# A decoder of two layers on one core: the projections of causal and full attention as three passes of rounded and rest parts

## The chip, the cores and the metric

The kernel runs on one core of one Trainium2 chip. The metric is the device time of one execution in microseconds, the median of the runs. TensorE (PE) multiplies, VectorE (DVE), ScalarE (ACT) and GpSimd (POOL) work element by element, and DMAs are issued from the queues of SyncE (SP) and POOL.

## The reference

The input x is 4 sequences of 512 tokens and 256 channels, in 32-bit floats. Six blocks follow each other, each on a layer norm of x and added to x:

```python
x = x + causal_attention(ln(x))         # 16 heads of 16, rope factor on q and k, projection + bias
x = x + geglu(ln(x), ctx)
x = x + routed_ffn(ln(x))               # 8 experts, top 2, and a shared one
x = x + full_attention(ln(x))           # 16 heads of 16
x = x + cross_attention(ln(x), ctx)     # softmax over the queries
x = x + routed_ffn2(ln(x))              # 8 experts of 1024
```

The two self attentions compute `qkv = x @ W.T + b`, softmax of `q k / 4`, times v, and `y @ W_out.T + b_out`. A projection in them is the product with `W` (256 x 768) or `W_out` (256 x 256).

## The kernel before

`attention` runs twice: once for the causal attention (tiles named l0a, four batches of 512 tokens), and once for full and cross attention together (l1a, batches 0 to 3 full, 4 to 7 cross). Each batch has four groups of four heads. A schedule written out by hand (`attention_slot`, L95) gives the order for all engines: one slot for a batch and group, in a slot eight steps j. Each step has the scores by key (`S`, L758) and, for a later group, the scores by query (`A`, L721), whose row maximum DVE takes (L539); ACT takes the exponential of S (L644). Scores use three PSUM buffers in turn: an S or A waits until the reader of the score three places before is done. `PV` (L783) multiplies probabilities with v; `Z` (L792) turns the result by tokens, DVE divides it (L547, L551), and `N` (L800) turns it back once for each pair of groups.

Everything else on PE shares one PSUM bank, `m_ps`: `take_m` makes the next writer wait for the reader of the last one. The work for the next batch sits in slots 0 and 1 of this one: `PREP` uses 0 and 1 transpose the normed x (L687; read by ACT, L604, into `xnT`), uses 2 to 5 are the four q and k chunks of 128 channels by 512 tokens (L698, two matmuls of 512 columns each), uses 6 and 7 are v (L707, two token tiles each, two matmuls of 256 columns for each tile). `OUT` (L809) is the output projection, two matmuls of 256 columns, read by DVE (L563), which adds it to x. It comes twice for each pair of groups, four times for a batch; pair 0 of a batch is projected in its slot 2, pair 1 in slot 0 of the next batch. So slot 0 has, one behind the other on `m_ps`: PREP 0 (step 3), N (step 4), PREP 1 (step 4), OUT (step 5), PREP 2 (step 6), OUT and PREP 3 (step 7).

A matmul on 32-bit operands is two records in the trace (each with a weight load). Operands that a rounding wrote as F32R are multiplied in one; the scores already work so, from `hi` and `lo` stacked along the contraction. Routed layers do three passes, hi times hi, hi times lo and lo times hi (helper at L1783 with 256 columns each).

A batch of index 0 is prepared before the loop: its PREP steps stand at the start of the stage, with score buffers in place of `m_ps`. Behind them SP issues the 48 DMAs that stack q (L393), then the row maxima of group 0 (L399); the first S waits for these.

## Time and profile before

| | us |
|---|---|
| median of 3 runs | 1979.07 (1970.0 to 1981.77) |
| the profiled execution's own time | 1973.59 |
| its span | 1971.8 |
| causal stage, first instruction to last | 9 to 316 |
| full attention, first to its last projections | 794 to 1152 |

The profiled execution has a mean granted TensorE clock of 0.878 of 2.4 GHz. In the 2.4 us between span and time nothing of the kernel runs. Of a view by windows, one line is a stretch of the span; the sums of engines overlap, so a stretch is as long as the chain of waits in it, not as the busiest engine. A record's length of a matmul holds its latency; the rate of a stream is the distance between starts.

### The profile page before, as it was taken

The numbers are of one execution on the slowest core, as the hardware profiler recorded it, in microseconds if no ns is written. First come the engines' busy times: TensorE is split into PE (matmuls) and PEld (weight loads), VectorE is DVE, ScalarE is ACT, GpSimd is POOL, SyncE is SP. The second block draws the span as 40 slices with busy tenths as digits, with TensorE's granted clock in tenths as the row PEclk, the third lists the DMA queues.
The fourth block names the chain that finished last, engine by engine and source line by source line (L and its number), as shares of the span: only waits on it lengthen the run. The fifth ranks groups of instructions, "written<-read, shape, count | busy, mean of one in ns | idle before, by whom it ended". The sixth has DMA issues, their size and how long they took to land. (4 is left out here: it accounts for less than half of the span.)

```text
span 1971.8 us, 32181 instructions
## 1 busy us (share of the span) xinstructions
PE 1569.6 (80%) x11072; PEld 1117.7 (57%) x11072; DVE 1191.7 (60%) x2003; ACT 932.7 (47%) x1745; POOL 609.2 (31%) x887
## 2 busy tenths in 40 slices
PE   4789986855969996378888977877760799999996
PEld 2455443555969996233333322322240799999996
DVE  3555553451458885377677467575743477787773
ACT  1344452121346663036546556466721466666662
POOL 5243420015004443624334343233015221222222
PEclk8799998956989998679999997676755899999998
DMA  5122211163058985434232222122015567777763
GB/s 142 25 52 51 49 34 33 53 168 112 28 155 235 232 232 127 117 77 96 45 80 60 61 41 52 34 55 40 9 44 174 158 202 213 219 204 201 210 193 80
DMA packets 211537, 216.56 MB, mean 110 GB/s; under 512 B 33393, under 2 KB 187378, under 8 KB 211346
## 3 DMA queue, kind: packets, MB, share of 16 engines
q1 hardware_dynamic: 176626, 175.10, 30.2%
q0 software_dynamic: 34752, 39.43, 11.3%
q8 instruction: 88, 1.44, 0.3%
q14 instruction: 71, 0.58, 0.1%
HBM read 139.48 MB, written 38.96 MB: 90 GB/s over the span
## 5 line engine op out<-in xcount | busy, mean ns | idle before, releaser
L638 ACT ACTIVATE l1a_sb_probs<-l1a_s_ps,l1a_sb_kmax 128x512 f32<-128x512 f32 x256 | 173.1, 684 | 95.9 <-issue 72.8
L1783 PE MATMUL l1m_xg_ps<-l1m_sb_xrows_hi,l1m_sb_hi 128*128 128x256 f32 x736 | 209.2, 284 | 1.4 <-DVE l1m_sb_xrows_lo L1705 1.4
L1783 PE MATMUL l1m_xg_ps<-l1m_sb_xrows_hi,l1m_sb_lo 128*128 128x256 f32 x736 | 208.9, 284 | 0.0
L1783 PE MATMUL l1m_xg_ps<-l1m_sb_xrows_lo,l1m_sb_hi 128*128 128x256 f32 x736 | 208.8, 284 | 0.0
L445 POOL DMA_DIRECT2D l1a_sb_kst<-l1a_sb_hi x256 | 125.5, 494 | 267.8 <-PE l1a_s_ps L758 236.3
L573 DVE TENSOR_REDUCE l1a_sb_kmax<-l1a_s_ps 128x2 f32<-128x1024 f32 x128 | 155.3, 1220 | 83.4 <-PE l1a_s_ps L758 83.3
L539 DVE TENSOR_REDUCE l1a_sb_mx<-l1a_s_ps 128x2 f32<-128x1024 f32 x128 | 154.1, 1219 | 75.2 <-PE l1a_s_ps L721 75.1
L1629 POOL DMA_INDIRECT sum_dram<-l1m_sb_xy,l1m_sb_xnote x46 | 79.8, 1734 | 322.5 <-DVE l1m_sb_xy L1755 315.5
L644 ACT ACTIVATE l1a_sb_probs<-l1a_s_ps 128x1024 f32<-128x1024 f32 x128 | 128.0, 1022 | 104.7 <-PE l1a_s_ps L758 104.5
L539 DVE TENSOR_REDUCE l0a_sb_mx<-l0a_s_ps 128x2 f32<-128x256 f32 (+3 forms) x128 | 103.4, 821 | 93.6 <-PE l0a_s_ps L732 92.2
L758 PEld LDWEIGHTS l1a_s_ps<-l1a_sb_qst,l1a_sb_kst 49*128 49x128 f32 (+1 forms) x512 | 51.6, 211 | 166.6 <-issue 102.6
L758 PE MATMUL l1a_s_ps<-l1a_sb_qst,l1a_sb_kst 49*128 49x512 f32 (+1 forms) x512 | 129.9, 534 | 18.3 <-issue 17.6
L1783 PEld LDWEIGHTS l1m_xg_ps<-l1m_sb_xrows_hi,l1m_sb_hi 128*128 128x128 f32 x736 | 141.9, 193 | 1.8 <-DVE l1m_sb_xrows_lo L1705 1.8
L1783 PEld LDWEIGHTS l1m_xg_ps<-l1m_sb_xrows_hi,l1m_sb_lo 128*128 128x128 f32 x736 | 142.0, 193 | 0.0
L1783 PEld LDWEIGHTS l1m_xg_ps<-l1m_sb_xrows_lo,l1m_sb_hi 128*128 128x128 f32 x736 | 141.9, 193 | 0.0
L1711 DVE TENSOR_TENSOR l1m_sb_lo<-l1m_sb_raw,l1m_sb_hi 128x512 fp32r<-128x512 f32 x184 | 119.9, 693 | 32.6 <-ACT l1m_sb_hi L1664 21.3
L783 PE MATMUL l1a_o_ps<-l1a_sb_probs,l1a_sb_vscaled 128*32 128x512 f32 x512 | 92.8, 805 | 58.0 <-DVE l1a_sb_vscaled L591 47.4
L644 ACT ACTIVATE l0a_sb_probs<-l0a_s_ps 128x1024 f32<-128x1024 f32 (+3 forms) x128 | 87.3, 698 | 78.3 <-PE l0a_s_ps L732 78.1
L1629 POOL DMA_INDIRECT sum_dram<-l0m_sb_xy,l0m_sb_xnote x46 | 79.4, 1726 | 137.6 <-DVE l0m_sb_xy L1755 127.6
L1664 ACT ACTIVATE l1m_sb_hi<-l1m_sb_raw 128x512 fp32r<-128x512 f32 x184 | 105.0, 620 | 16.4 <-DMA l1m_sb_raw<-in_l1m_w 16.2
L1783 PE MATMUL l1m_xy_ps<-l1m_sb_hi,l1m_sb_xh_hi 128*128 128x256 f32 x368 | 106.7, 290 | 2.8 <-issue 2.8
L1783 PE MATMUL l0m_xg_ps<-l0m_sb_xrows_hi,l0m_sb_hi 128*128 128x256 f32 x368 | 105.5, 287 | 2.7 <-DVE l0m_sb_xrows_lo L1705 2.7
(332 smaller groups left out, 4199.1 us busy)
## 6 DMA issues: line engine op xcount, KB each, us to landing
l1m_sb_raw<-in_l1m_w SPq DMA_DIRECT2D x184, 256.0 KB
l0m_sb_raw<-in_l0m_w SPq DMA_DIRECT2D x96, 256.0 KB
l1m_sb_raw<-in_l1m_w SPq DMA_DIRECT2D x23, 1024.0 KB
l0m_sb_raw<-in_l0m_w SPq DMA_DIRECT2D x24, 512.0 KB
l1a_sb_qst<-l1a_sb_hi SPq DMA_DIRECT2D x256, 32.0 KB, 2.3
l1a_sb_kst<-l1a_sb_hi POOLq DMA_DIRECT2D x256, 32.0 KB, 2.0
rows_dram<-const_blank SPq DMA_DIRECT2D x2, 2967.0 KB, 24.1
l0m_sb_xrows<-rows_dram SPq DMA_DIRECT2D x23, 258.0 KB, 4.2
```

Source lines behind the costliest of these rows:

```text
L445: pool.dma_start(in_stack(kst, p, e, n), in_part(source, i, p, e)).then_inc(kstacked[p], 16)
L539: dve.tensor_reduce(mx[:, g, qt, 2 * p:2 * p + 2], buffer("A", b, g, j)[:, :, 0:last], AX.X, ALU.max).then_inc(a_max.sem, 1)
L573: dve.tensor_reduce(kmax[:, n % 4, :], buffer("S", b, g, j)[:, :, :], AX.X, ALU.max, negate=True).then_inc(kmax_done.sem, 1)
L638: ins = act.activation(probs[:, n % 8, e, :], at[:, e, :], ACT.Exp, bias=kmax[:, n % 4, e:e + 1], accum_out=zsum[:, n % 4, e:e + 1])
L644: act.activation(probs[:, n % 8, :, c0:T], at[:, :, c0:T], ACT.Exp, scale=SCALE).then_inc(exp_done.sem, 1)
L758: ins = pe.matmul(at[:, e, c0:T], kst[rows, p, kt * P:(kt + 1) * P], qst[rows, p, c0:T], start=True, stop=not causal)
L783: ins = pe.matmul(o_ps[32 * i:32 * i + 32, c0:T], (vscaled if cross else vaug)[:, kt, GH * g + i, :], probs[:, (8 * g + 2 * kt + i // 2) % ...
L1629: pool.indirect_dma_start(total, bass.IndirectOffsetOnAxis(ap=note[:, (2 * i + k) % 4, t, 0:1].bitcast(U32), axis=0), y[:, k % 2, t, :], None,
L1664: ins = act.activation(two_chunks(hi, k % 2, f), two_chunks(raw13, n, f), ACT.Copy)
L1711: ins = dve.tensor_tensor(two_chunks(lo, k % 2, f), two_chunks(raw13, n, f), two_chunks(hi, k % 2, f).bitcast(F32), ALU.subtract)
L1783: ins = pe.matmul(at, s, m, start=n == 0, stop=n == len(passes) - 1)
```

## The change

For causal and full batches (cross is untouched):

- Once for each stage, ACT rounds the four pieces of the weights to F32R (`whi`, `wout_hi`) and DVE takes the difference from the original (`wlo`, `wout_lo`). Both stand ahead of the stage's first copies of x.
- The transposed x is read twice: ACT copies it rounded to `xhi`, DVE subtracts that from the PSUM bank into `xlo`. The same with the attention's output: `ohi` by ACT, `olo` by DVE (step N). The bank is free for the next writer after DVE, not after ACT.
- Each projection is three passes on PE in place of one 32-bit product: hi hi, lo hi, hi lo.
- `one_row`, from which the rows of ones in `kst` are filled, is 64 long and not 512; the two DMAs have pieces of 64 elements.

```diff
+                          "split": None if kind == "cross" else
+                          [(sb(f"w{part}{n}", [P, CC, 3 * D], F32R), sb(f"wout_{part}{n}", [P, NG // 2, D], F32R))
+                           for part in ("hi", "lo")],
...
-        xnT = sb("xnT", [P, CC, T])
+        xnT = sb("xnT", [P, CC, T]) if has_cross else None
+        xhi, xlo = sb("xhi", [P, CC, T], F32R), sb("xlo", [P, CC, T], F32R)
...
-        oT = sb("oT", [P, T])
+        ohi, olo = sb("ohi", [P, T], F32R), sb("olo", [P, T], F32R)
...
-        one_row = sb("one_row", [1, T], F32R)
+        one_row = sb("one_row", [1, 64], F32R)
...
+        w_split = sem("w_split")
+        w_rest = sem("w_rest")
+        x_rest = steps("x_rest", CC, 0)
+        o_rest = steps("o_rest", NG // 2, 0)
...
+            if use < 2 and kinds[b] != "cross":
+                return x_rest, b, use
...
+        def weight_piece(b, n):
+            (whi, out_hi), (wlo, out_lo) = part(b)["split"]
+            if n < CC:
+                return part(b)["wqkv"][:, n, 0:2 * D], whi[:, n, 0:2 * D], wlo[:, n, 0:2 * D]
+            if n == CC:
+                return part(b)["wqkv"][:, :, 2 * D:], whi[:, :, 2 * D:], wlo[:, :, 2 * D:]
+            return part(b)["wout"][:, :, :], out_hi[:, :, :], out_lo[:, :, :]
...
-                sp.dma_start(kst[64 * e + 48:64 * e + 49, :, :].bitcast(F32),
-                             one_row[0:1, :].bitcast(F32).unsqueeze(1).to_broadcast([1, NPAIR, T])
+                sp.dma_start(kst[64 * e + 48:64 * e + 49, :, :].bitcast(F32).rearrange("o p (a t) -> o (p a) t", t=64),
+                             one_row[0:1, :].bitcast(F32).unsqueeze(1).to_broadcast([1, NPAIR * T // 64, 64])
...
+                if use < 2 and kinds[b] != "cross":
+                    if b % B == 0 and use == 0:
+                        for n in range(4):
+                            dve.wait_ge(w_split, b // B * 4 + n + 1)
+                            raw, rounded, rest = weight_piece(b, n)
+                            dve.tensor_tensor(rest, raw, rounded.bitcast(F32), ALU.subtract).then_inc(w_rest, 1)
+                    m_act.wait(dve, b, use)
+                    dve.tensor_tensor(xlo[:, use, :], product(b, use), xhi[:, use, :].bitcast(F32), ALU.subtract
+                                      ).then_inc(x_rest.sem, 1)
...
+            def rest_back(b, g, _):
+                oT_copied.wait(dve, b, g // 2)
+                out_ready.wait(dve, b, g // 2 * 2 - 1)
+                dve.tensor_tensor(olo[:, :], m_ps[:, :], ohi[:, :].bitcast(F32), ALU.subtract).then_inc(o_rest.sem, 1)
...
-                 "A": row_max, "Z": invert})
+                 "A": row_max, "Z": invert, "N": rest_back})
...
+                    if b % B == 0 and use == 0 and kinds[b] != "cross":
+                        act.wait_ge(part(b)["in"], 5 * 16)
+                        for n in range(4):
+                            raw, rounded, _ = weight_piece(b, n)
+                            act.activation(rounded, raw, ACT.Copy).then_inc(w_split, 1)
...
-                    act.activation(xnT[:, use, :], product(b, use), ACT.Copy).then_inc(m_act.sem, 1)
+                    to = xnT if kinds[b] == "cross" else xhi
+                    act.activation(to[:, use, :], product(b, use), ACT.Copy).then_inc(m_act.sem, 1)
...
-                act.activation(oT[:, :], m_ps[:, :], ACT.Copy).then_inc(oT_copied.sem, 1)
+                act.activation(ohi[:, :], m_ps[:, :], ACT.Copy).then_inc(oT_copied.sem, 1)
...
+            def three_passes(at, chunks):
+                passes = [(s[i], m[j]) for s, m in chunks for i, j in ((0, 0), (1, 0), (0, 1))]
+                for n, (s, m) in enumerate(passes):
+                    ins = pe.matmul(at, s, m, start=n == 0, stop=n == len(passes) - 1)
+                return ins
...
-                    m_act.wait(pe, b, 1)
+                        if not cross:
+                            pe.wait_ge(w_rest, b // B * 4 + 4)
+                    if cross:
+                        m_act.wait(pe, b, 1)
+                    else:
+                        x_rest.wait(pe, b, 1)
...
-                    for c in range(CC):
+                    cols = slice(CHUNK[i] * P, (CHUNK[i] + 1) * P)
+                    if not cross:
+                        (whi, _), (wlo, _) = w["split"]
+                        ins = three_passes(at, [((whi[:, c, cols], wlo[:, c, cols]), (xhi[:, c, :], xlo[:, c, :]))
+                                                for c in range(CC)])
+                    for c in range(CC if cross else 0):
...
+                        if not cross:
+                            (whi, _), (wlo, _) = w["split"]
+                            rows = slice(t * P, (t + 1) * P)
+                            ins = three_passes(cols, [((xhi[:, c, rows], xlo[:, c, rows]),
+                                                       (whi[:, c, 2 * D:], wlo[:, c, 2 * D:])) for c in range(CC)])
+                            continue
...
-                                            start=not cross and c == 0, stop=c == CC - 1)
+                                            start=False, stop=c == CC - 1)
...
-                take_m(oT_copied, b, g // 2)
+                take_m(o_rest, b, g // 2)
...
-                pair, src = g // 2, ox if kinds[b] == "cross" else oT
-                (ox_copied if kinds[b] == "cross" else oT_copied).wait(pe, b, pair)
+                pair, cross = g // 2, kinds[b] == "cross"
+                (ox_copied if cross else o_rest).wait(pe, b, pair)
...
-                    ins = pe.matmul(m_ps[:, (t % 2) * D:(t % 2 + 1) * D], src[:, t * P:(t + 1) * P],
+                    rows = slice(t * P, (t + 1) * P)
+                    if not cross:
+                        (_, out_hi), (_, out_lo) = part(b)["split"]
+                        ins = three_passes(m_ps[:, (t % 2) * D:(t % 2 + 1) * D],
+                                           [((ohi[:, rows], olo[:, rows]), (out_hi[:, pair, :], out_lo[:, pair, :]))])
+                        continue
+                    ins = pe.matmul(m_ps[:, (t % 2) * D:(t % 2 + 1) * D], ox[:, rows],
```

On DVE, in the third full batch, slot 0 (`mx` is the row maximum, `on` the divided output, `x_sb` the addition of OUT). Before:

```order
L487 TENSOR_SCALAR l1a_sb_xn<-x_sb,l1a_sb_mv,l1a_sb_rstd 128x256 x4
L539 TENSOR_REDUCE l1a_sb_mx<-l1a_s_ps 128x2
L547 RECIPROCAL l1a_sb_rz<-l1a_o_ps 128x16
L551 TENSOR_TENSOR l1a_sb_on<-l1a_o_ps,l1a_sb_rz 128x4x64
L539 TENSOR_REDUCE l1a_sb_mx<-l1a_s_ps 128x2 x2
L563 TENSOR_TENSOR x_sb<-l1a_m_ps,x_sb 128x512
L539 TENSOR_REDUCE l1a_sb_mx<-l1a_s_ps 128x2
```

and of the change:

```order
L507 TENSOR_SCALAR l1a_sb_xn<-x_sb,l1a_sb_mv,l1a_sb_rstd 128x256 x4
L568 TENSOR_REDUCE l1a_sb_mx<-l1a_s_ps 128x2
L576 RECIPROCAL l1a_sb_rz<-l1a_o_ps 128x16
L580 TENSOR_TENSOR l1a_sb_on<-l1a_o_ps,l1a_sb_rz 128x4x64
L518 TENSOR_TENSOR l1a_sb_xlo<-l1a_m_ps,l1a_sb_xhi 128x512
L568 TENSOR_REDUCE l1a_sb_mx<-l1a_s_ps 128x2
L587 TENSOR_TENSOR l1a_sb_olo<-l1a_m_ps,l1a_sb_ohi 128x512
L518 TENSOR_TENSOR l1a_sb_xlo<-l1a_m_ps,l1a_sb_xhi 128x512
L568 TENSOR_REDUCE l1a_sb_mx<-l1a_s_ps 128x2
L597 TENSOR_TENSOR x_sb<-l1a_m_ps,x_sb 128x512
```

Three subtractions (L518, L587, L518) now stand between the divided output and the row maximum of step 5, with one row maximum among them.

On ACT, at the start of the causal stage (`hi` is the rounding of q and k chunks). Before:

```order
L604 ACT_TABLE_LOAD
L604 ACTIVATE l0a_sb_xnT<-l0a_s_ps 128x512 x2
L622 ACTIVATE l0a_sb_hi<-l0a_sb_qk 128x512 x4
L613 ACTIVATE l0a_sb_v<-l0a_s_ps 128x512 x2
L627 ACTIVATE l0a_sb_mT<-l0a_m_ps 4x512
```

and of the change:

```order
L641 ACTIVATE l0a_sb_whi<-l0a_sb_wqkv 128x512 x2
L641 ACTIVATE l0a_sb_whi<-l0a_sb_wqkv 128x2x256
L641 ACTIVATE l0a_sb_wout_hi<-l0a_sb_wout 128x512
L644 ACTIVATE l0a_sb_xhi<-l0a_s_ps 128x512 x2
L662 ACTIVATE l0a_sb_hi<-l0a_sb_qk 128x512 x4
```

Four roundings of weights stand ahead of the two copies of x. On DVE the four differences stand in the same way, behind the normed x and ahead of `xlo`:

```order
L507 TENSOR_SCALAR l0a_sb_xn<-x_sb,l0a_sb_mv,l0a_sb_rstd 128x256 x4
L516 TENSOR_TENSOR l0a_sb_wlo<-l0a_sb_wqkv,l0a_sb_whi 128x512 x2
L516 TENSOR_TENSOR l0a_sb_wlo<-l0a_sb_wqkv,l0a_sb_whi 128x2x256
L516 TENSOR_TENSOR l0a_sb_wout_lo<-l0a_sb_wout,l0a_sb_wout_hi 128x512
L518 TENSOR_TENSOR l0a_sb_xlo<-l0a_s_ps,l0a_sb_xhi 128x512 x2
L532 SCALAR_TENSOR_TENSOR l0a_sb_qk<-l0a_s_ps,l0a_sb_bqk,const_rope 128x512
```

So the first q chunk on PE has eight instructions of ACT and DVE more ahead of it, on two engines side by side, and two more for `xlo`.

## Rows read from the trace of the kernel before

**Rows 1.** Part 1 of the page: busy us, share of the span, instructions.

```profile
PE 1569.6 (80%) x11072; PEld 1117.7 (57%) x11072; DVE 1191.7 (60%) x2003; ACT 932.7 (47%) x1745; POOL 609.2 (31%) x887
```

**Rows 2.** Windows: busy us (instructions) by engine, granted clock, DMA; slots named 0.

```profile
core 0: us, PE busy (x) PEld busy (x) DVE busy (x) ACT busy (x) POOL busy (x), PEclk, DMA share, GB/s
130.70:155.40 24.70, 22.10 (x171) 10.84 (x170) 13.41 (x23) 8.56 (x16) 13.84 (x23) 0.93 0.15 32
198.70:221.70 23.00, 20.43 (x172) 10.43 (x168) 13.41 (x22) 8.54 (x16) 13.79 (x23) 1.00 0.18 37
997.40:1021.95 24.55, 20.44 (x107) 8.38 (x106) 18.20 (x24) 11.30 (x14) 14.87 (x25) 1.00 0.18 37
```

**Rows 3.** Waits, 840 to 1080 us: who waited for whom, us, times, longest.

```profile
PE l1a_s_ps L721 <- ACT l1a_sb_probs L644: 15.4, 21, 0.8
```

**Rows 4.** Timeline: start us, length, instruction; start of the causal stage, weight loads.

```profile
18.20 0.34 PEld L698 LDWEIGHTS l0a_s_ps<-l0a_sb_xnT,l0a_sb_wqkv 128*128 128x128 f32 x1 [0.52 <-issue]
...
22.47 0.34 PEld L698 LDWEIGHTS l0a_s_ps<-l0a_sb_xnT,l0a_sb_wqkv 128*128 128x128 f32 x1 [0.52 <-issue]
...
24.13 0.19 PEld L698 LDWEIGHTS l0a_s_ps<-l0a_sb_xnT,l0a_sb_wqkv 128*128 128x128 f32 x1 [0.24 <-issue]
...
26.27 0.19 PEld L698 LDWEIGHTS l0a_s_ps<-l0a_sb_xnT,l0a_sb_wqkv 128*128 128x128 f32 x1 [0.24 <-issue]
```

**Rows 5.** Timeline of the same start, all engines.

```profile
15.36 2.34 POOL L434 TENSOR_TENSOR x_sb<-x_sb,l0a_sb_bo 128x1024 f32<-128x1024 f32 x1 [2.46 <-DMA l0a_sb_wout<-in_l0a_wout]
...
17.22 10.07 PE L698 MATMUL l0a_s_ps<-l0a_sb_xnT,l0a_sb_wqkv 128*128 128x512 f32 x16 [0.78 <-ACT l0a_sb_xnT L604]
...
21.09 0.75 DVE L503 SCALAR_TENSOR_TENSOR l0a_sb_qk<-l0a_s_ps,l0a_sb_bqk,const_rope 128x512 f32<-128x512 f32 x1 [6.68 <-PE l0a_s_ps L698]
...
23.32 0.59 SPq L393 DMA_DIRECT2D l0a_sb_qst<-l0a_sb_hi  x1
...
27.13 3.62 PE L707 MATMUL l0a_s_ps<-l0a_sb_wqkv,l0a_sb_xnT 128*128 128x256 f32 x16
...
53.74 2.48 SPq L399 DMA_DIRECT2D l0a_sb_qst<-l0a_sb_mT  x4
```

**Rows 6.** Timeline of the second routed layer: halves, and passes of 256 columns.

```profile
1799.39 1.14 ACT L1670 ACTIVATE l1m_sb_hi<-l1m_sb_raw 128x512 fp32r<-128x512 f32 x2
1799.47 2.49 DVE L1717 TENSOR_TENSOR l1m_sb_lo<-l1m_sb_raw,l1m_sb_hi 128x512 fp32r<-128x512 f32 x4
...
1800.11 0.28 PE L1783 MATMUL l1m_xg_ps<-l1m_sb_xrows_lo,l1m_sb_hi 128*128 128x256 f32 x1
...
1801.19 0.28 PE L1783 MATMUL l1m_xg_ps<-l1m_sb_xrows_lo,l1m_sb_hi 128*128 128x256 f32 x1
```

**Rows 7.** Timeline: start of the full attention.

```profile
800.05 2.35 POOL L434 TENSOR_TENSOR x_sb<-x_sb,l1a_sb_bo 128x1024 f32<-128x1024 f32 x1 [2.52 <-DMA l1a_sb_wout<-in_l1a_wout]
...
801.83 8.60 PE L698 MATMUL l1a_s_ps<-l1a_sb_xnT,l1a_sb_wqkv 128*128 128x512 f32 x16 [0.78 <-ACT l1a_sb_xnT L604]
...
842.48 0.80 PE L758 MATMUL l1a_s_ps<-l1a_sb_qst,l1a_sb_kst 49*128 49x512 f32 x2 [17.62 <-issue]
```

**Rows 8.** Timeline: slot 0 of the full attention's third batch.

```profile
1001.72 0.60 ACT L604 ACTIVATE l1a_sb_xnT<-l1a_m_ps 128x512 f32<-128x512 f32 x1 [1.13 <-PE l1a_m_ps L687]
...
1002.24 0.42 DVE L551 TENSOR_TENSOR l1a_sb_on<-l1a_o_ps,l1a_sb_rz 128x256 f32<-128x256 f32 x1
...
1002.72 0.66 PE L800 MATMUL l1a_m_ps<-const_ident,l1a_sb_on 128*128 128x128 f32 x4 [0.37 <-DVE l1a_sb_on L551]
...
1003.41 0.60 ACT L661 ACTIVATE l1a_sb_oT<-l1a_m_ps 128x512 f32<-128x512 f32 x1 [0.17 <-PE l1a_m_ps L800]
...
1004.30 0.66 PE L687 MATMUL l1a_m_ps<-const_ident,l1a_sb_xn 128*128 128x128 f32 x4
...
1005.74 1.10 PE L809 MATMUL l1a_m_ps<-l1a_sb_wout,l1a_sb_oT 128*128 128x256 f32 x4
```

**Rows 9.** Lines, DVE, 840 to 1080 us: busy us, mean ns, idle before.

```profile
L563 DVE TENSOR_TENSOR x_sb<-l1a_m_ps,x_sb 128x512 f32<-128x512 f32 x11 | 7.5, 686 | 0.3 <-PE l1a_m_ps L809 0.3
```

## The prediction, made before the changed kernel had run

> **What bounds the kernel now.** I read the page first for the busy shares, then windows of single slots, the waits of the full attention, and last the timeline where the change puts its instructions. Over the whole span PE is busy 80% [rows 1], but the span is several stages, and only the causal and full attention are changed. In their slots 0 PE is busy 20.43 of 23.00 us (causal) and 20.44 of 24.55 us (full); DVE follows with 13.41 and 18.20 us [rows 2]. So PE's stream sets the pace there, and an engine beside it matters where PE has to wait for it. Such waits exist: PE waited 15.4 us, in 21 pieces of at most 0.8 us, for the exponentials of ACT [rows 3]. The two starts are another thing. In the causal one SP issues the stacking of q without a break from 23.32 us, and the row maxima are issued only at 53.74 us [rows 5]; in the full one the first scores by key start at 842.48 us after 17.62 us of idle PE [rows 7]. What delays the first q chunk there delays all behind it, and a faster PE in the rest of the start gives nothing, since SP's queue hides it.
>
> **What PE gains.** A 32-bit matmul is two records. At the high clock, weight loads of those with 512 columns stand 0.428 us apart ((26.27 - 24.13) / 5 steps, the rows between left out [rows 4]); with 256 columns 16 records take 3.62 us, 0.216 us each once the length of the last is taken off [rows 5]. A pass on rounded operands with 256 columns takes 0.12 us ((1801.19 - 1800.11) / 9 [rows 6]). A pass with 512 columns over all 128 rows is in no row. Its lower bound is half a 32-bit record of 512 columns, 0.214 us; its upper bound twice the pass of 256, 0.24 us. The upper counts the fixed part of a pass twice, so I take 0.22 us.
> - A q or k chunk: 4 x 0.428 = 1.71 us becomes 6 x 0.22 = 1.32 us: 0.39 less.
> - A PREP use of v: 8 x 0.216 = 1.73 us becomes 12 x 0.12 = 1.44 us: 0.29 less.
> - An OUT: 4 x 0.216 = 0.86 us becomes 6 x 0.12 = 0.72 us: 0.14 less.
>
> In the loop are the chunks of six batches (three causal, three full), 24, and 12 uses of v; OUT comes 4 times in each of 8 batches. That is 9.4 + 3.5 + 4.5 = **17.4 us**. I count all of it: while a chunk runs the other engines drain and wait for PE, so what a chunk gives back moves everything behind it.
>
> The Trainium skill ("TensorE: Matmul & The Clock Gate", section "Back-to-back issue gap") gives for a lone warm matmul a gap of columns / 2.4 + 2.5 ns. That is 0.109 us for 256 columns and 0.216 us for 512; the sum would be 21.5 us in place of 17.4. The row has 0.12 for 256, so the measurement decides there; for 512 no run here shows it yet.
>
> **What the starts cost.** The weights have landed at 15.36 us, when POOL's bias, which waits for the last of them, begins [rows 5]. ACT now rounds four pieces first, at 0.57 us (two in 1.14 [rows 6]), to 17.65 us, and then copies x twice at 0.60 [rows 8], to 18.85. DVE's four differences (four in 2.49 us [rows 6]) run beside, one piece behind; its two subtractions of x, at 0.69 us like the other DVE operation that reads this bank [rows 9], end at about 19.8 us. PE started its first chunk at 17.22 us [rows 5]: 2.6 us later. The chunk itself runs at the low clock; there 32-bit records stand 0.854 us apart ((22.47 - 18.20) / 5 [rows 4]), 3.4 us for four, and six passes at twice 0.22 us take 2.6: 0.8 less. The first q chunk is 1.8 us late, and with it SP's queue. For the full attention the same from 800.05 us: ready at 804.5 and not 801.83 us [rows 7], 1.9 us late in the end. Together **3.7 us**. Of the other edits at the start, `one_row` as pieces of 64 elements costs nothing: SP is idle until the first stacking DMA, and its rows are first needed after the row maxima. If that cover were gone, it would be two DMA issues.
>
> **What the shared bank costs.** In slot 0 of a batch, `m_ps` is handed from PREP 0 to N to PREP 1 to OUT within two steps, and each of the first three is now released by DVE behind ACT. In the full attention's third batch [rows 8]:
> - N started at 1002.72, just behind DVE's divided output (1002.24 + 0.42). Now DVE first does `xlo`, 1002.66 to 1003.35, and N has to wait for it: 0.7 late.
> - ACT's copy for N moves from 1003.41 to 1004.1, ends at 1004.7, and `olo` at 1005.4. PREP 1 started at 1004.30, so it is 1.1 late.
> - Its transposes take 0.6 to 0.7, ACT's copy 0.6, `xlo` 0.7: the bank is free at 1007.4. OUT started at 1005.74, so it is **1.6** late in all; step 5's scores fit in between.
>
> There are four such slots, the slots 0 of batches 1 and 2 of either attention: 6.4 us. Where full meets cross, two more slots have only the middle part, about 0.4 each: 0.8. In slot 2 N stands alone: ACT's copy and 0.69 us of DVE end just when OUT comes, one step of scores and a PV later, which hides it; without that cover it would be 0.7 for each. At the end of the causal stage nothing covers `olo`: 0.7. Together **7.9 us**. DVE's other work grows by 4 x 0.69 = 2.8 us for each batch; its idle time in the slots (6.35 us of 24.55 in the full slot 0 [rows 2]) takes that. What is late next in slot 0 is the row maximum of step 5 behind `xlo`, with three score buffers ahead of it.
>
> **The sum**: 17.4 gained, 3.7 + 7.9 = 11.6 lost, 5.8 us faster. Against the profiled execution's 1973.6 us this is 1967.8; against the median of 1979.1 it is 1973.3. Three runs spread over 11.8 us, and the profiled one lies in their lower half, so I take **1970**.
>
> **The rivals.**
> - *The bank's turns are hidden* (chance 0.15). For it: PE has idle time in every slot, 2.57 us in the causal slot 0 [rows 2], and a late N may only use it up. Against: the waits are one behind the other on PE's own order. Time: -17.4 + 3.7, that is 1959.9 from the profiled run, 1965.4 from the median.
> - *DVE's queue comes onto the path* (0.14), the case that ends slower. Each of the 28 subtractions of x and output behind the starts (4 in each of 8 batches, less 4 in the starts) would be paid in full, because a row maximum stands behind it, and the scores need the buffer which that maximum frees. 28 x 0.69 = 19.3 in place of 7.9 us: +5.6, 1979.2 to 1984.7. It decides once the maxima are late by more than the three buffers cover, that is when DVE's idle time in a slot is below what PE can wait. For it: DVE's 18.20 us in the full slot 0; against: with 2.1 more it is still 20.3 of 24.5 [rows 2].
> - *The clock falls in the waits* (0.14). The causal slots 0 with a granted clock of 0.93 and 1.00 differ by 24.70 to 23.00 us: 1.7 us for one stretch at 1.2 GHz [rows 2], in which PE had stood behind DVE's addition. If the six slots with longer waits each get one, +10.2: 1978 to 1983.5. The Trainium skill (same page, section "HAM oscillation — how this bites in real kernels") has idle gaps between bursts as the cause of a fall; by that rule the longer waits make it likelier. The causal slot at 0.93 agrees, the full one at 1.00, with like waits, does not.
> - *A pass with 512 columns is no faster than a 32-bit record* (0.05), so that the change doesn't do what it says: 0.428 us, a chunk 0.86 longer in place of 0.39 shorter, 24 times: +24, 1998 to 2003. The pass of 256 speaks against it.
>
> **How the numbers follow.** The forecast has 0.52. With its bounds (0.214 and 0.24 for the pass: 0.9 more or 2.9 less gained; from 0 to twice the cost of bank turns) and the two bases it spans 1959 to 1981. The range for 8 in 10 is **1957 to 1988**: it takes in the hidden turns but for their lower edge, DVE's queue and the clock, and leaves out the slow pass. A change of under 1% (19.8 us) can't be told from none here. Faster than 1959.3 us is the lower edge of the first rival with a good clock: 0.08. Slower than 1998.9 us is the slow pass and the worst of the clock: 0.06. Within 1%: 0.86.
>
> **What would show it.** Chunks of six records whose loads are 0.21 to 0.24 us apart; N in slots 0 about 0.7 us later behind the divided output, with PE idle on `xlo` or `olo` before N, PREP 1 and OUT; no such idle before OUT in slot 2; first stacking DMA of q about 1.8 us later in both starts. With slots cut as in [rows 2], from one transposition of row maxima to the next, the two of slots 0 at full clock hold three chunks and two OUT (1.5 us less) and the bank's turns (1.6 more), so they stay as long as they are; the slots 1 behind them, with one chunk and two uses of v, get 1.0 us shorter. I am wrong if the row maxima rather than the bank hold PE up, if the granted clock in slots 0 is below 0.9, or if stages that the change doesn't touch move by more than the gain.

## The result, and the profile after

The changed kernel takes **1988.99 us** (median of 20 runs, 1975.65 to 2000.55) and the kernel before, beside it, 1971.27 us (20 runs, 1964.85 to 1991.59). The ratio is 1.0076, with a 95% interval of 1.0055 to 1.0098: 11 to 19 us slower. The forecast was 1970 in a range up to 1988, so the time lies 1 us outside, and the change went the other way.

The profiled execution of the changed kernel took 1988.2 us. The page's first part, with the row of the granted clock; against [rows 1] PE is 3.7 us less busy and DVE 33 us more:

```profile
span 1986.3 us, 32627 instructions
## 1 busy us (share of the span) xinstructions
PE 1565.9 (79%) x11264; PEld 1140.7 (57%) x11264; DVE 1224.6 (62%) x2043; ACT 937.8 (47%) x1753; POOL 609.2 (31%) x887
...
PEclk8799997956989999679999986767765799999998
```

The **causal start**, timeline (columns as in [rows 5]). The weights have landed when ACT starts to round them:

```profile
16.90 1.67 ACT L641 ACTIVATE l0a_sb_whi<-l0a_sb_wqkv 128x512 fp32r<-128x512 f32 x3 [6.65 <-DMA l0a_sb_wout<-in_l0a_wout]
16.95 2.36 POOL L454 TENSOR_TENSOR x_sb<-x_sb,l0a_sb_bo 128x1024 f32<-128x1024 f32 x1 [4.52 <-DMA l0a_sb_wout<-in_l0a_wout]
17.56 3.49 DVE L516 TENSOR_TENSOR l0a_sb_wlo<-l0a_sb_wqkv,l0a_sb_whi 128x512 fp32r<-128x512 f32 x3 [3.63 <-ACT l0a_sb_whi L641]
...
20.98 0.68 DVE L516 TENSOR_TENSOR l0a_sb_wout_lo<-l0a_sb_wout,l0a_sb_wout_hi 128x512 fp32r<-128x512 f32 x1
21.58 1.28 DVE L518 TENSOR_TENSOR l0a_sb_xlo<-l0a_s_ps,l0a_sb_xhi 128x512 fp32r<-128x512 f32 x2
...
23.00 0.77 PE L719 MATMUL l0a_s_ps<-l0a_sb_xhi,l0a_sb_whi 128*128 128x512 f32 x1 [7.05 <-DVE l0a_sb_xlo L518]
...
28.25 0.54 SPq L413 DMA_DIRECT2D l0a_sb_qst<-l0a_sb_hi  x1
```

The first chunk starts at 23.00 and not at 17.22 us, SP's first stacking DMA at 28.25 and not at 23.32 [rows 5]. Asked for L516 alone, the trace gives its fastest, middle and slowest: one of the differences takes 2.29 us, the others 0.68:

```profile
L516 DVE TENSOR_TENSOR l0a_sb_wlo<-l0a_sb_wqkv,l0a_sb_whi x3: 678/679/2291, 17.6 to 20.4; 128x512 fp32r<-128x512 f32 x3
```

That one starts at 17.56, while POOL adds the bias until 19.31, and ends at 19.85, 0.54 us behind POOL. In the start of the full attention one takes 2.30 us in the same way. Passes of 512 columns, weight loads at the high clock, ten steps in 2.33 us, 0.233 each (0.22 was taken):

```profile
28.15 0.19 PEld L719 LDWEIGHTS l0a_s_ps<-l0a_sb_xhi,l0a_sb_wlo 128*128 128x128 f32 x1
28.38 0.19 PEld L719 LDWEIGHTS l0a_s_ps<-l0a_sb_xlo,l0a_sb_whi 128*128 128x128 f32 x1
...
30.48 0.19 PEld L719 LDWEIGHTS l0a_s_ps<-l0a_sb_xlo,l0a_sb_whi 128*128 128x128 f32 x1
```

**Inside the loops**, PE's waits in the causal attention: the two groups on `xlo` and two on `olo` are new.

```profile
PE l0a_m_ps L862 <- DVE l0a_sb_xlo L518: 2.1, 2, 1.0
PE l0a_m_ps L719 <- DVE l0a_sb_xlo L518: 1.5, 2, 0.8
PE l0a_m_ps L719 <- DVE l0a_sb_olo L587: 1.5, 1, 1.5
...
PE l0a_m_ps L733 <- DVE l0a_sb_olo L587: 0.4, 1, 0.4
```

And by windows: the loop of the causal attention (from its first scores by key to its last output projection), that of the full one (to its last transposition of row maxima), and the cross stage behind it. First a second profile of the kernel before (before_again, below), then the changed kernel. Columns as in [rows 2]; the granted clock is the third value from the end, 0.97 and 0.94 in the causal loops:

```profile
57.53:314.59 257.06, 229.97 (x2336) 126.45 (x2337) 141.02 (x230) 119.21 (x191) 88.90 (x165) 0.97 0.19 39
840.58:1107.02 266.44, 229.96 (x1259) 95.93 (x1260) 193.34 (x244) 139.38 (x163) 102.00 (x185) 0.96 0.32 69
1107.02:1442.54 335.52, 257.03 (x1112) 89.59 (x1111) 213.11 (x350) 210.92 (x553) 96.26 (x186) 0.76 0.20 40
```

```profile
62.91:322.23 259.32, 227.83 (x2420) 136.50 (x2420) 149.83 (x244) 119.51 (x191) 89.23 (x165) 0.94 0.20 38
851.13:1116.73 265.60, 224.58 (x1331) 102.44 (x1331) 200.83 (x256) 139.34 (x163) 102.25 (x185) 0.96 0.31 70
1116.73:1460.18 343.45, 262.87 (x1121) 91.44 (x1119) 219.30 (x352) 211.49 (x553) 96.59 (x186) 0.74 0.19 40
```

The loops do no more than stay level, and the cross stage, whose code is unchanged, is 8 us longer. In all three the length and the granted clock have to be read together, so the table below gives for each kernel the length of a stage and, behind the stroke, how many us of it TensorE was granted 1.2 GHz, added up from the trace's record of the clock (a window's clock gives it too, coarsely: 2 x (1 - 0.94) x 259 = 31). In the table every stage ends where its last product starts (the full loop: its last transposition of row maxima); the windows above end up to 0.8 us before that.

```
profiled     causal  causal      full   full        cross        ratio to before
execution    start   loop        start  loop        stage        (95% interval)
before       57.5    257.6/16.9  68.2   269.1/23.8  334.3/153.6
before_again 57.5    257.8/17.7  67.9   266.4/19.7  336.3/160.4
changed      62.9    259.3/30.6  70.9   265.6/23.4  344.2/177.5  1.0076 (1.0055, 1.0098)
after_again  63.1    257.3/25.2  70.7   268.7/30.0  342.4/161.2  1.0075 (1.0046, 1.0103)
starts_only  61.8    257.2/16.3  71.7   268.3/21.9  333.3/150.2  1.0019 (0.9998, 1.0039)
qkv_only     63.2    257.1/21.6  71.7   272.1/39.6  334.7/154.3  1.0044 (1.0021, 1.0066)
out_only     57.0    259.5/24.0  66.7   267.6/21.3  347.0/187.7  1.0038 (1.0012, 1.0063)
light_start  58.6    255.4/19.9  67.3   265.6/23.4  331.9/144.1  1.0001 (0.9972, 1.0030)
no_meeting   60.5    259.2/30.5  69.6   270.8/34.8  343.6/167.3  1.0060 (1.0033, 1.0088)
light_qkv    58.3    256.3/19.6  67.7   269.4/30.1  350.6/204.8  1.0032 (1.0007, 1.0056)
early_rel.   59.6    269.5/44.2  67.9   274.4/29.6  341.6/174.1  1.0110 (1.0076, 1.0143)
causal_only  63.1    259.3/30.6  66.9   266.2/17.6  344.6/187.7  1.0029 (0.9999, 1.0058)
full_only    56.9    260.0/24.5  72.1   271.4/39.2  350.8/201.4  1.0031 (0.9998, 1.0063)
padded       63.9    263.2/20.8  71.3   274.4/27.9  350.2/194.6  1.0134 (1.0090, 1.0177)
no_rest      61.9    253.3/28.0  70.2   261.9/24.2  345.3/184.3  0.9998 (0.9968, 1.0028)
before_warm  57.3    257.4/16.6  68.1   265.5/16.1  316.8/54.6   0.9891 (0.9858, 0.9924)
light_warm   58.0    258.1/25.9  66.8   265.4/23.5  310.6/34.1   0.9908 (0.9867, 0.9950)
```

The start of the full attention is counted from the last product of the stage before it. Four kernels (after_again, no_meeting, light_qkv, early_release) ran on another chip, on which the stages between the two attentions are some 30 us shorter; their ratios are to runs of before on that chip. **How the table is read**: profiles of the same loop differ by the low clock alone. The causal loop of the change is 255.4 us with 19.9 low and 259.3 with 30.6: 0.36 us for each. The full one, 265.6/23.4 and 271.4/39.2: 0.37. The cross stage, 331.9/144.1 and 350.8/201.4: 0.33. Whole executions say the same: among the 19 to 35 runs of one kernel on one chip the time rises by 0.34 to 0.38 us for each us at the low clock (their mean clock and span give it). So lengths are compared at the same time at the low clock, and the rest is its price.

**Where the clock falls.** Cut from one transposition of row maxima to the next, as in [rows 2], nearly all low stretches in the middle of a loop lie in the slots 0. In those of batches 1 and 2 the five profiles of either loop with 32-bit products have 4 such stretches in 20 slots; the four with the changed kernel's order (changed, after_again, no_meeting and the half that has it) have 18 in 16. Nine of the 18 begin 5.1 to 6.3 us into the slot, within 0.4 us of the start of N, which had waited 1.05 us for `xlo`. In the third full batch of the changed kernel:

```profile
1004.10:1007.50 3.40, 1.67 (x13) 0.88 (x11) 3.37 (x8) 2.06 (x3) 3.40 (x8) 1.00 0.53 110
1007.46 0.94 PE L862 MATMUL l1a_m_ps<-const_ident,l1a_sb_on 128*128 128x128 f32 x4 [1.06 <-DVE l1a_sb_xlo L518]
1007.70:1011.00 3.30, 3.30 (x16) 1.21 (x14) 1.43 (x2) 0.60 (x1) 3.29 (x4) 0.50 0.23 46
```

The other nine begin at 16.7 to 19.8 us, beside PE's wait for DVE's addition of OUT, where the 32-bit kernels' four lie too (15.3 to 17.1). In the causal loop that wait is longer where OUT is three passes, with the rests (1.44 us) or without them (before, then no_rest, below); in the full one it is 0.78 us in both kernels.

```profile
213.96 1.55 PE L698 MATMUL l0a_m_ps<-l0a_sb_xnT,l0a_sb_wqkv 128*128 128x512 f32 x3 [1.28 <-DVE x_sb L563]
213.84 0.50 PE L713 MATMUL l0a_m_ps<-l0a_sb_xhi,l0a_sb_whi 128*128 128x512 f32 x1 [1.43 <-DVE x_sb L589]
```

### The profile page after: what moved, and what is told of

The parts are those of the page before. It is cut to its first block and busy times, and to the rows that moved or that the text cites. A ratio compares the mean times of both kernels' runs of the same rounds, so it can differ in the third digit from the quotient of the medians.

```text
span 1986.3 us, 32627 instructions
## 1 busy us (share of the span) xinstructions
PE 1565.9 (79%) x11264; PEld 1140.7 (57%) x11264; DVE 1224.6 (62%) x2043; ACT 937.8 (47%) x1753; POOL 609.2 (31%) x887
## 5 line engine op out<-in xcount | busy, mean ns | idle before, releaser
L845 PE MATMUL l1a_o_ps<-l1a_sb_probs,l1a_sb_vscaled 128*32 128x512 f32 x512 | 97.2, 842 | 61.0 <-DVE l1a_sb_vscaled L625 49.0
L820 PE MATMUL l1a_s_ps<-l1a_sb_qst,l1a_sb_kst 49*128 49x512 f32 (+1 forms) x512 | 131.7, 541 | 16.8 <-issue 16.3
L1732 ACT ACTIVATE l1m_sb_hi<-l1m_sb_raw 128x512 fp32r<-128x512 f32 x184 | 105.0, 620 | 16.4 <-DMA l1m_sb_raw<-in_l1m_w 16.2
```

The lines of the kernel that those rows point to most:

```text
L820: ins = pe.matmul(at[:, e, c0:T], kst[rows, p, kt * P:(kt + 1) * P], qst[rows, p, c0:T], start=True, stop=not causal)
L845: ins = pe.matmul(o_ps[32 * i:32 * i + 32, c0:T], (vscaled if cross else vaug)[:, kt, GH * g + i, :], probs[:, (8 * g + 2 * kt + i // 2) % ...
L1732: ins = act.activation(two_chunks(hi, k % 2, f), two_chunks(raw13, n, f), ACT.Copy)
```

## The experiments

**The start alone** (starts_only): the kernel before, with the weights split but not used.

```diff
                     if b % B == 0 and i == 0:
                         pe.wait_ge(w["in"], 5 * 16)
+                        if not cross:
+                            pe.wait_ge(w_rest, 4)
```

> The kernel before, with nothing new but the split of the weights at the two starts: all projections stay 32-bit and read the whole weights; the rounded and the rest parts are made, the first q chunk waits for them, and nothing reads them. Theory 1 (the starts were too cheap in the forecast): the changed kernel's trace has its first scores by key 5.5 us later in the causal start and some 3 us later in the full one; without the copies and rests of x this kernel keeps 4 to 5 and 2.5 to 3.5 of it, 7 to 8 us in all, so a median near 1979, with the loops and the cross stage as long as before. Theory 2 (a shifted start alone also changes in which stretches TensorE's clock is low, and the cross stage pays for it): the same 7 to 8 us and up to 10 more, near 1989. The forecast's own working would be 3 us: 1974.

The first scores by key came 4.3 us later in the causal start, 3.5 in the full one; the loops and the cross stage stayed. The profiled execution is 3.8 us longer (the stage between was 2 us shorter), the ratio 1.0019. Theory 1 holds in sizes by stage, and a shift in time doesn't by itself lengthen the cross stage.

**One part alone** (qkv_only, out_only).

```diff
-                take_m(o_rest, b, g // 2)
+                take_m(oT_copied, b, g // 2)
```

> The changed kernel with its output projection back at 32-bit products and the bank released by ACT's copy as before; q, k and v stay in three passes. Theory 1 (terms as forecast for the loops): OUT loses 4.5 us of gain, and slots 0 get back the part of the bank's turns that olo makes, 0.7 to 0.9 us in each of four, and 0.7 at the causal end: near no difference to the changed kernel, 1987 to 1990. Theory 2 (every olo is paid in full on the path, 16 of 0.69 us): 4.5 less 11, so 1982. Theory 3 (it is the clock's phase): anything within 10 us of the changed kernel, with a cross stage that is not 343 us long.

> The kernel before with only the output projection in three passes; of the weights only the output's are split, behind the last v use of the start, where nothing waits for them. Theory 1: the starts stay (first scores by key within 1 us of before), 4.5 us gained in OUT, 0.9 x 4 and 0.7 lost at olo: 1970 to 1972, as before. Theory 2 (each olo in full): 11 lost and 4.5 gained, 1978. Theory 3 (clock): a cross stage of up to 10 us more than before's 333.6 us without any change at the starts.

8.7 and 7.5 us over before; both miss their theory 1. Theory 2 of qkv_only has its median (1983.3 against 1982), but not its loops: at equal time at the low clock they are 1.1 (causal) and 0.2 us (full) longer than the changed kernel's and not 3 shorter. Each has a loop with more low clock than before's (39.6 us in the full one, 24.0 in the causal one). out_only keeps its starts (57.0 and 66.7 us) as expected and still loses: 12.7 us of its profile are in the cross stage, with 34 us more at the low clock. That spoke for the clock, without telling why.

**The start in another order** (light_start, no_meeting).

```diff
-                    if b % B == 0 and use == 0 and kinds[b] != "cross":
-                        act.wait_ge(part(b)["in"], 5 * 16)
-                        for n in range(4):
+                if b == 0 and use in (2, 6):
+                    act.wait_ge(part(b)["in"], 5 * 16)
+                    for n in range(4) if use == 2 else (4, 5):
...
+                if b == 0 and g == 3:
+                    bias(b, g)
```

The last two lines, in POOL's step for v, are no_meeting, together with a return that leaves out the bias where the step of the first batch had it; light_start has them too.

> The changed kernel with its start in another order: x is copied and its rest taken before the weights are split; the weights are split by chunk, so the first q chunk waits for one piece of 256 columns and not for four of up to 512; v's and the output's pieces come behind the q and k chunks; POOL adds the bias of the first batch behind its v groups and not while DVE takes the differences. Theory 1 (order and the meeting of DVE and POOL make the start's cost): the first scores by key come 4 to 5 us earlier than in the changed kernel in the causal start and 2 to 3 in the full one: 1981 to 1983. If the landing of the weights rather than the order sets it, 1 us each: 1987. Theory 2 (clock): the cross stage again differs from 343 us by several us, either way.

> The changed kernel with one edit: POOL adds the bias of the first batch behind its v groups of the start, so that it doesn't run while DVE takes the differences of the weights. Theory 1 (the meeting of the two engines doubled three of the four differences): each of the four takes 0.6 to 0.7 us, the first scores by key come 1.5 us earlier in each start, 3 us in all. Rival (the differences are long because they start cold or read what ACT has just written): 1.16 us for each of three as in the changed kernel, and no gain.

In no_meeting the three differences of the q, k and v weights take 1.89 us in place of 3.49:

```profile
16.38 1.67 ACT L645 ACTIVATE l0a_sb_whi<-l0a_sb_wqkv 128x512 fp32r<-128x512 f32 x3 [5.50 <-DMA l0a_sb_wout<-in_l0a_wout]
17.04 1.89 DVE L520 TENSOR_TENSOR l0a_sb_wlo<-l0a_sb_wqkv,l0a_sb_whi 128x512 fp32r<-128x512 f32 x3 [2.48 <-ACT l0a_sb_whi L645]
...
20.88 0.77 PE L723 MATMUL l0a_s_ps<-l0a_sb_xhi,l0a_sb_whi 128*128 128x512 f32 x1 [4.30 <-DVE l0a_sb_xlo L522]
```

So POOL's bias had held DVE up for 1.6 us: shown. The first scores by key come 2.4 us earlier than in the changed kernel in the causal start (the weights landed 0.5 us earlier there) and 1.1 us earlier than in after_again in the full one: the 3 us of theory 1. With light_start, whose first scores by key come 4.3 and 3.6 us earlier than in the changed kernel (theory 1 on order), the first chunk starts at 17.90 us, and behind it the scores by key at 58.6 and, in the full start, 0.9 us earlier than before:

```profile
16.64 1.32 ACT L645 ACTIVATE l0a_sb_whi<-l0a_sb_wqkv 128x256 fp32r<-128x256 f32 x4
16.77 0.69 DVE L523 TENSOR_TENSOR l0a_sb_xlo<-l0a_s_ps,l0a_sb_xhi 128x512 fp32r<-128x512 f32 x1 [0.16 <-ACT l0a_sb_xhi L649]
17.38 0.75 DVE L520 TENSOR_TENSOR l0a_sb_wlo<-l0a_sb_wqkv,l0a_sb_whi 128x256 fp32r<-128x256 f32 x2
...
17.90 0.77 PE L724 MATMUL l0a_s_ps<-l0a_sb_xhi,l0a_sb_whi 128*128 128x512 f32 x1 [1.79 <-DVE l0a_sb_wlo L520]
```

The start's 8 us were its order, and the kernel is level with before (ratio 1.0001), 15 us under the changed one by the two ratios; the intervals leave 7 to 22. The part beyond 8 is clock: its runs have 12 us more at 1.2 GHz than before's beside them, those of after_again 25.

**Variants of the light start** (light_qkv, early_release).

```diff
+                    act.activation(xnT[:, use, :], product(b, use), ACT.Copy).then_inc(m_act.sem, 1)
+                    m_act.wait(act, b, use)
+                    act.activation(xhi[:, use, :], xnT[:, use, :], ACT.Copy).then_inc(x_high.sem, 1)
```

> The light start (light_start) with the output projection back at 32-bit products: q, k and v in three passes. Theory 1: against light_start OUT loses 4.5 us and olo's turns of the bank give back 4.3, so 1971 to 1973 and level with before. Theory 2 (olo is paid in full, 16 of 0.69 us): 6.5 us under light_start, 1965. Theory 3 (clock): the stages away from the edit differ by more than the stages with it.

> The light start with both banks' turns shortened: ACT copies x (and the divided output) from the bank to SBUF in 32 bit, which frees the bank; it rounds from there in a second copy, and DVE takes the rest from SBUF. Theory 1 (waits for the shared bank cost 1.6 us in each of four slots 0 and some at the causal end): 5 to 6 us under light_start, near 1966, and slots 0 at full clock 1.2 to 1.6 us shorter. Rival (ACT has no room: four more copies of 0.6 us for each batch, in front of the exponentials that PE waits for): up to 32 x 0.6 less what it gains, slots 0 no shorter, 1972 to 1982.

light_qkv is 6 us over before, light_start level: no gain from leaving `olo` out, theory 2 is out, and once more the stage away from the edit is the long one. At equal low clock its loops are 1.0 and 1.3 us longer than light_start's: near theory 1's none, and not 3 us shorter. early_release is 21 us over before, so theory 1 falls. It is also more than the rival's 10, and the cost isn't at the exponentials:

```profile
PE l0a_m_ps L731 <- DVE l0a_sb_olo L592: 9.5, 8, 2.7
PE l0a_s_ps L797 <- ACT l0a_sb_probs L693: 8.5, 20, 1.1
```

The output projection has to wait for `olo` itself, which is now a copy later: 9.5 us in 8 waits, and 8.9 more in the full loop. The clock goes with it: in the slots 0 of batches 1 and 2 four low stretches begin at 10.0 to 13.0 us, beside or behind OUT's wait of 2.7 us for `olo`, and none at 5 to 6 us, where N no longer waits for `xlo`. Freeing a bank earlier is no use where the value made from it is what comes next.

**One attention alone** (causal_only, full_only), and a second profile of either kernel.

> Three passes in the causal attention only; the full attention keeps its 32-bit products and its start. Theory 1 (terms add by stage): the causal start costs 5.5 us, the causal loop gives back 0 to 1, the rest is as before: 5 to 6 us over before. Theory 2 (the change in the full attention is what makes the cross stage behind it longer): here the cross stage stays at 331 to 335 us and the mean granted clock is at most 0.002 under before's. Rival (the cross stage's length is thrown by any change ahead of it): a cross stage of 340 us or more, and 10 to 14 us over before.

> Three passes in the full attention only; the causal one as before. Theory 1: start +3 us, full loop -3.5 us, the rest as before: level with before. Theory 2 (the full attention's change lengthens the cross stage): the cross stage at 340 us or more, the mean granted clock 0.004 to 0.006 under before's, 7 to 10 us over before.

> The changed kernel once more, unchanged, for a second profile beside the same runs of before. Theory 1 (the lower clock in the cross stage belongs to the kernel): mean granted clock 0.865 to 0.868, a cross stage of 341 to 346 us, a median 13 to 17 us over before. Theory 2 (the profiled execution fell so by chance): the median stays 13 to 17 us over before, but the cross stage is back at 331 to 335 us and the time sits elsewhere.

> The kernel before once more, unchanged, for a second profile. If the cross stage's length is chance of the execution, it lies anywhere from 330 to 350 us here; the causal loop at 256.5 to 258 and the full one at 265.5 to 269 us, as in the four profiles of 32-bit loops so far.

The halves cost 1.0029 and 1.0031, together 12 us, about the whole. causal_only is the 6 us over before of its theory 1, but with the rival's long cross stage; full_only, 6 us over, lies between its two theories. Theory 2 falls: causal_only, with nothing changed in the full attention, has a cross stage of 344.6 us. Its causal loop has 30.6 us at the low clock like the changed kernel's. The two further profiles came out near the first ones. (after_again's mean clock, 0.875, is above the range expected, but on its chip before's is 0.880.)

**PE's work against PE's waits** (padded, no_rest).

```diff
+                for width in more:
+                    pe.matmul(at[:, 0:width], passes[0][0], passes[0][1][:, 0:width], start=True, stop=True)
```

For a chunk `more` is (512, 256).

> The changed kernel with PE's saving put back: in front of the three passes stand passes that are overwritten (512 and 256 columns for a q or k chunk, 256 for each half of v, 256 for an OUT), so that PE works as long as with 32-bit products; the rests and their waits stay. Working: 12 x 0.32 + 6 x 0.29 + 16 x 0.14 = 7.8 us more work in each loop. Theory W (PE's longer waits for the rests make the clock fall): the time at the low clock in the causal loop stays at 25 to 31 us and the loops are 7 to 8 us longer than the changed kernel's, causal 265 to 267 us; 14 to 16 us over it. Theory S (the shorter work between the waits does it): the low clock falls back to 13 to 17 us in the causal loop, which takes 260 to 262 us; 4 to 8 us over the changed kernel.

> The changed kernel without the rests of x and of the divided output: DVE doesn't take them (the two tiles stay zero, so the products lack those parts), PE makes all three passes, and the bank is released by ACT's copy as before. The splits of the weights stay. Theory W: the bank's turns (4 us in each loop) and the low clock both go: the causal loop at 13 to 17 us of low clock and 248 to 251 us long, the full one 259 to 262. Theory S: the turns go, the low clock stays at 25 to 31 us in the causal loop: 253 to 256 us, full 262 to 265. If the turns cost nothing, the causal loop stays at 257 to 259 us.

At 15 us of low clock the causal loop is 256.8 us with 32-bit products, 253.6 in the changed kernel, 261.1 in padded (263.2 less 5.8 x 0.36) and 248.6 in no_rest (253.3 less 13.0 x 0.36). So the passes save 8.2 us, the rests cost 5.0. The full loop at 22 us: 267.9 (mean of five), 265.5 (mean of four), 272.2 and 261.1: 6.8 saved, 4.4 lost. padded agrees from the other side: it is 7.5 and 6.7 us over the changed loops (7.8 of work put back), and 4.3 over the 32-bit ones, the rests' cost.

The low clock itself fits neither theory alone. padded's causal loop has 20.8 us of it, within the 32-bit kernels' 16.3 to 24.5; no_rest's has 28.0, within the changed ones' 25.2 to 30.6: theory S, and no_rest's two stretches in the slots 0 both begin beside the longer wait for the addition. In the full loop no_rest has none in the slots 0 of batches 1 and 2, where the four changed profiles have 11, and padded still has one at 5.7 us, beside the wait for `xlo`: theory W. These are single profiles. Over all its runs neither kernel gets before's clock back (520 and 524 us at 1.2 GHz, before's beside them 488). By the ratios padded is 11 us over the changed kernel, between the two theories.

**PE kept at work** (before_warm, light_warm): in the cross stage 36 products that nothing reads.

```diff
+                if cross and (g, kt) in ((1, 2), (1, 3), (2, 0), (2, 2), (2, 3), (3, 0), (3, 1), (3, 2), (3, 3)):
+                    last, lb, lstep = m_reader[0]
+                    last.wait(pe, lb, lstep)
+                    pe.matmul(m_ps[:, :], const["ident"][:, :], const["rope"][:, :], start=True, stop=True)
```

> The kernel before with work added that nothing reads: in the cross stage, at 9 of the 16 products with the probabilities of a batch, PE first multiplies two constant tiles into the shared bank while nobody holds it (32 bits, 512 columns, 0.86 us at full clock; 36 in all, 31 us of work), mostly where it would wait for the scaled v. Theory 1 (the cross stage is as long as TensorE's clock makes it; over the profiles so far a microsecond at the low clock costs 0.4 us): the clock of the stage rises from 0.77 to 0.85 or more, and the stage falls from 333 to 310 to 328 us in spite of the work. Rival (DVE's maxima and ACT's exponentials set it): the stage takes 334 to 365 us whatever the clock does.

> The light start (light_start: all projections in three passes) with the same added work in the cross stage. Theory 1 (clock): what light_start has gained ahead of the cross stage, 7 us by its profile, is no longer given back there; cross stage and clock as in the kernel before with the same work, and the median 5 to 8 us under that kernel's, so under before by 10 to 25. Rival: the cross stage is 334 to 365 us long, and the kernel slower than before.

The cross stage of before, then of before_warm, then of light_warm:

```profile
1111.60:1445.18 333.58, 254.03 (x1112) 88.84 (x1111) 213.16 (x350) 210.85 (x553) 96.25 (x186) 0.77 0.20 41
```

```profile
1105.10:1421.14 316.04, 261.33 (x1184) 91.59 (x1183) 212.88 (x350) 211.66 (x553) 96.45 (x186) 0.91 0.21 43
```

```profile
1107.07:1416.99 309.92, 251.80 (x1192) 89.22 (x1191) 214.45 (x352) 211.12 (x553) 96.23 (x186) 0.94 0.21 44
```

With more instructions the clock of the stage rises from 0.77 to 0.91, PE's waits for the scaled v fall from 47.4 us to 26.1, and the stage is 18 us shorter, as theory 1 had it; the whole kernel is 1.1% faster than before. That is the fastest version here, and it beats both kernels. light_warm is level with it (0.9908 against 0.9891) and not 5 to 8 us faster: its loops have 16.7 us more at the low clock than before_warm's, 6.0 us at 0.36, about what its passes and its start save. The Trainium skill ("TensorE: Matmul & The Clock Gate", section "HAM oscillation — how this bites in real kernels") has idle gaps between bursts as the cause of a falling clock; here the trace agrees, filling nine gaps a batch took 99 of 154 us at the low clock away.

## Why the prediction was wrong

Two steps failed: the starts were priced at 3.7 us and cost 8.5, and the clock was left out of the sum and cost 8.2 or more. With the starts alone put right, 1 us of the 5.8 is left; with the clock too it is 7 us lost, and the passes and the bank add 4. One of the prediction's own signs came true: the cross stage, which the change doesn't touch, moved by 8 to 10 us, more than the gain.

- **What PE gains** (17.4 us): 15.0 by no_rest. The mechanism was right, the pass of 512 columns mis-sized: 0.233 and not 0.22 us, for 24 chunks of six 1.8 less (15.6).
- **What the shared bank costs** (7.9 us): 9.4 by no_rest, 5.0 and 4.4. The mechanism was right, the size 1.5 us too small. In the full slot of [rows 8], counted from its transposition of row maxima, N is 0.69 us later (0.7 forecast); the causal OUT of the third batch starts 9.29 us behind that mark and not 7.39, 1.9 later (1.6). The slots 1 are 0.9 to 1.0 us shorter (1.0 forecast). A causal slot 0 without low clock is 23.75 and not 23.01 us (0.1 forecast).
- **What the starts cost** (3.7 us): this step failed. 5.5 in the causal start, 3 in the full one. 2.6 us of delay of the first chunk were forecast and 5.8 came: 1.6 because DVE stood behind POOL's bias, which [rows 5] had shown beginning at that very moment, and 1.5 because the weights landed at 16.90 and not 15.36. The price of 0.62 us for a difference came from a row that has no addition of POOL beside it. The landing differs between executions, whatever the kernel (16.2 in before_again, 16.9 in full_only, whose causal start is as before, 16.4 to 16.9 in changed ones); before, the copies of x hid most of it. The prediction's single figure had no room for a later one.
- **The clock** was a rival with 0.14 and 10.2 us, and stood at nothing in the sum: this step failed too. It came true beside the forecast, not in its stead. Over the four profiles with the changed kernel's order the causal loop spends 29.2 us at 1.2 GHz where five with 32-bit products have 18.4, the full one 31.9 where five have 19.8: 10.8 and 12.0 at 0.36, **8.2 us**. (With the light start it is less, 19.9 and 25.9, 23.4 and 23.5.) Its mechanism, a fall in the longer waits, is what half of the falls in slots 0 show (9 of 18 beside N's wait for `xlo`; no kernel without rests of x has one there). The other half lie where the clock fell before too, beside the wait for the addition, but more often. In the causal loop PE is done sooner with OUT, DVE's addition behind it is no faster, and so that wait grows from 1.28 to 1.44 us. In the full one it doesn't grow, and why the clock falls there more often stays open. That the length of a wait makes the difference is argued from these places, not tested by itself.
- *DVE's queue on the path* and *a pass no faster* did not happen: no row maximum waits behind a rest for long (PE's waits for maxima are 1.1 and 3.2 us), and the passes are faster.

The sum with what was measured: -15.0 + 9.4 + 8.5 + 8.2 = 11.1 us, against 15 (ratio 1.0076, 11 to 19). The clock's term comes from single profiles; the mean clocks of whole runs give it too. after_again's six runs have 25 us more at 1.2 GHz than before's 19 on that chip (clocks of 0.874 and 0.880), 8.9 us at 0.36, which with the other terms' 2.9 makes 11.8; the means of the times are 11.6 apart. The changed kernel's 20 runs have 529 us at 1.2 GHz (0.867), before's on the three other chips 488 to 498: 11 to 15 us at 0.36, so that 14 to 18 us in all are explained. (no_rest fits worst: its time is 4 us under such a sum.) What the loops don't show of this lies mostly in the cross stage: it takes 341.6 us or longer in ten of the twelve profiles with any of the change in a loop (light_warm left out), and 333.3 to 336.3 in the three of before and starts_only, all with the same code there. Why the clock is lower there stays open.

## What to carry to other kernels

Where PE already waits for others, a change can be paid back in PE's clock, by the waits that it adds and perhaps by the work that it takes away: price a saving at both clocks, and add that term to the sum instead of keeping it as a rival. Ask of each new operation at a start which other engine is just then adding in SBUF, and order it so that what the first product needs comes first. A stage whose granted clock is far below 1 can be worth more than the change at hand: here 36 products for nothing gave 22 us.

## What the hardware showed beyond what was expected

- **DVE stands still while POOL adds.** Besides the differences of 2.29 and 2.30 us, one scaling of v in the changed kernel's cross stage, 0.225 us elsewhere, took 4.13 us, through the whole of POOL's bias, and PE stood idle 3.85 us ahead of the product that reads it:

```profile
1312.88 4.13 DVE L625 TENSOR_TENSOR l1a_sb_vscaled<-l1a_sb_v,l1a_sb_rzsum 128x64 f32<-128x64 f32 x1
...
1314.56 2.35 POOL L454 TENSOR_TENSOR x_sb<-x_sb,l1a_sb_bo 128x1024 f32<-128x1024 f32 x1
...
1317.11 1.94 PE L845 MATMUL l1a_o_ps<-l1a_sb_probs,l1a_sb_vscaled 128*32 128x512 f32 x8 [3.85 <-issue]
```

  It ends 0.1 us behind POOL's addition; in the profile of before no such scaling took over 0.228 us. The Trainium skill ("SBUF — State Buffer", section "SBUF: two separate sides") has DVE and GpSimd share one pair of ports as an exclusive lock: a DVE operation with two inputs in SBUF and a GpSimd operation that reads SBUF block each other for a whole instruction. The difference and the move of the bias in no_meeting agree. The scaling began 1.7 us before the bias, which the rule alone doesn't explain.
- **The clock's low time varies from run to run.** Over the 20 runs of the changed kernel the mean granted clock goes from 0.860 to 0.875 and the time from 2000.55 to 1975.65 us: 66 us less at 1.2 GHz, 24 of the 25 us of spread at 0.36 each.
